# A graph and expert kernel: the gate moves into the second graph layer, and lots are gathered from lists instead of scattered to a buffer

## The reference

```python
x = x + _L0_gnn_ref(_layernorm(x), edge_index, edge_type_8, ...)   # two rgcn layers, relu between
x = x + _L0_ffn_ref(_layernorm(x)[None], Wg, bg, W1, b1, W2, b2)[0]

gate_logits = xf @ Wg + bg
top_w, top_i = jax.lax.top_k(gate_logits, 2)
top_w = jax.nn.softmax(top_w, axis=-1)
for e in range(E):                       # E = 8, H = 1024
    h = jax.nn.gelu(xf @ W1[e] + b1[e], approximate=False)
    out = out + w_dense[:, e:e + 1] * (h @ W2[e] + b2[e])
```

## Time and profile before

| what | us |
|---|---|
| median of 3 runs | 2932.98 (2931.1 to 2933.84) |
| span of the profiled execution | 3487.9 |
| setup and layer 1, until its last tile is out | 1383 |
| layer 2, until its last tile is out | 2665 |
| first matmul of the first lot | 2861 |
| end of the expert stage | 3488 |

### The profile page before, as it was taken

One profiled execution on the slowest core, in us unless ns is written; L12 is line 12 of the kernel. 1 busy time (PEld: TensorE's weight loads), 2 busy tenths in 40 slices (PEclk: granted clock), 3 DMA queues, 4 the chain that ended last, 5 costly groups with the idle time before them and its releaser, 6 DMA issues.

```text
span 3487.9 us, 82172 instructions
## 1 busy us (share of the span) xinstructions
PE 2472.0 (71%) x19212; PEld 1832.7 (53%) x19213; DVE 1780.8 (51%) x4984; ACT 1225.2 (35%) x2344; POOL 1862.5 (53%) x1980
## 2 busy tenths in 40 slices
PE   1346787678687786346776587687877428999999
PEld 0113565356365564114564365465656327888887
DVE  7324455345355454124454354354545338787777
ACT  5202343134243342012343143152432126555554
POOL 1666566655655554666556656655563543333333
PEclk9557999589799898557998798798997559999999
DMA  6223323233332232223333333333335234322222
GB/s 216 80 83 112 88 87 91 85 87 89 87 88 87 86 89 64 86 84 97 98 104 97 94 100 99 94 105 95 101 100 163 102 115 132 96 73 71 71 70 59
DMA packets 165489, 333.24 MB, mean 96 GB/s; under 512 B 36078, under 2 KB 102346, under 8 KB 165288
## 3 DMA queue, kind: packets, MB, share of 16 engines
q0 software_dynamic: 91632, 247.48, 24.1%
q1 hardware_dynamic: 39912, 41.03, 4.0%
q10 hardware_dynamic: 33872, 43.92, 3.9%
HBM read 285.39 MB, written 49.07 MB: 96 GB/s over the span
## 4 chain that ended last, share of the span: by engine, by line
PE 44%; issue 22%; DVE 10%; another core or an unknown queue 9%; DVEq 7%; SPq 2%; ACT 2%; DMA 1%; ACTq 0%; POOLq 0%; POOL 0%
PE more_banks L1408 13%; PE sum_banks L1384 9%; PE sum_banks L1385 7%; PE more_banks L1535 4%; PE sum_banks L1535 3%; PE more_banks L1400 3%; PE sum_banks L1545 3%; DVEq L1044 3%; DVEq L1041 2%; DVE sels L1044 2%; DVEq L1027 1%; DVE stage L1079 1%; DVE sels L1036 1%; PE sum_banks L1426 1%
## 5 line engine op out<-in xcount | busy, mean ns | idle before, releaser
L509 POOL DMA_INDIRECT ring<-table,tabs x1584 | 1526.9, 964 | 1046.4 <-SPq L399 670.0
L1384 PE MATMUL sum_banks<-ring,sels 128*128 x2348 | 726.6, 311 | 630.1 <-issue 420.1
L1408 PE MATMUL more_banks<-weights,stage 128*128 128x256 f16 x5292 | 919.1, 290 | 22.0 <-issue 21.4
L1385 PE MATMUL sum_banks<-ring,sels 128*128 x2348 | 732.2, 313 | 41.5 <-issue 38.7
L1384 PEld LDWEIGHTS sum_banks<-ring,sels 128*128 128x128 f16 (+1 forms) x2348 | 242.4, 103 | 928.2 <-issue 896.9
L683 ACT ACTIVATE stage<-sum_banks,inv 128x256 f16<-128x256 f32 x784 | 328.1, 473 | 789.5 <-issue 384.9
L1408 PEld LDWEIGHTS more_banks<-weights,stage 128*128 128x128 f16 x5292 | 531.1, 104 | 135.3 <-issue 37.1
L1036 DVE SCALAR_TENSOR_TENSOR sels<-lane,win_off,tabs 128x256 f16<-128x256 f16 x792 | 349.4, 482 | 422.1 <-remote 181.9
L654 ACT ACTIVATE stage<-more_banks 128x1024 f16<-128x1024 f16 x392 | 402.0, 1026 | 419.1 <-remote 405.6
L1044 DVE TENSOR_SCALAR sels<-lane,win_off,tabs 128x128 f16 x780 | 260.6, 334 | 495.8 <-issue 339.6
L1079 DVE SCALAR_TENSOR_TENSOR stage<-sum_banks,inv,stage 128x256 f16<-128x256 f32 x784 | 347.0, 479 | 57.2 <-issue 40.2
(11 more groups left out here) (319 smaller groups left out, 2407.5 us busy)
## 6 DMA issues: line engine op xcount, KB each, us to landing
ring<-table,tabs POOLq DMA_INDIRECT x1584
weights<-L_ffn_W ACTq DMA_DIRECT2D x96, 178.5 KB
stage<-L_ffn_W ACTq DMA_DIRECT2D x16, 1024.0 KB, 5.0
edge_work<-lot_in SPq DMA_DIRECT2D x54, 260.0 KB
table<-edge_work ACTq DMA_DIRECT2D x49, 128.0 KB
lot_in<-sels SPq DMA_DIRECT2D x8, 260.0 KB
weights<-L_gnn_W SPq DMA_DIRECT2D x2, 1024.0 KB, 8.3
weights<-L_gnn_W ACTq DMA_DIRECT2D x2, 1024.0 KB
```

The costliest lines, as they stand in the source:

```text
L509: pool.indirect_dma_start(ring_rows[:, b % RING, 0:2 * D], None, tables[layer], bass.IndirectOffsetOnAxis(row_tab[:, b:b + 1], 0)).then_in ...
L1384: pe.matmul(to[:, 0:D + 1], hot, ring_row[:, ds(at + D, D + 1)], start=first, stop=last, skip_group_check=True)
L1385: return pe.matmul(to[:, 0:D], hot, ring_row[:, ds(at, D)], start=False, stop=last, skip_group_check=True)
L1408: return [pe.matmul(ps_out[par], rows[:, xp * KD + k, :], w16[:, wp, k, r * D:(r + 1) * D], start=part == PART_ORDER[0] and n == 0, stop=p ...
```

## The change

The scatter and its buffer go. The normed rows are written once, in node order, to `z_dram` by plain transfers, and POOL gathers each lot with two indirect transfers from lists of node numbers. The lists are made on the chip: a place within an expert is split into a low part (0 to 127) and a column; for each of 49 x 2 tile and choice pairs DVE marks both as one-hot matrices, ACT scales one copy by the row in the tile and POOL another by the tile, and PE multiplies them into PSUM (`ps_nth`, `ps_tile`), where the list of node numbers stands.

The rows z, their transposes, the gate product and the logits are made tile by tile inside the loop of layer 2, three to four tiles behind (`gate_tiles` in the place of `graph_tiles`, with four tiles ahead of the loop). Choice and places are done for 45 tiles at once and then for the last 4.

```diff
+        def gate_tiles(eng, body):
+            for t in range(4):
+                body(t, t % 2, t)
+            with eng.Fori(2, PAIRS) as i:
+                body(i * 2, 0, 4)
+                body(i * 2 + 1, 1, 4)
+            body(TILES - 1, 0, 4)
@@ PE, in a couple of layer 2
+                    if layer == 1 and k == 0 and age >= 4:
+                        z_transposes(t - 4, par, 1 - par, t - 2)
                     regs, at, need, end = load_couple(c)
+                    if layer == 1 and k == 2 and age >= 4:
+                        gate(t - 4, par, ps_sum[slot][1][:, GATE_AT:GATE_AT + X])
@@ ACT, in a tile of layer 2
+                            if k == 0 and age >= 3:
+                                deviation(t - 3)
+                            if k == 0 and age >= 4:
+                                z_columns(t - 4, par, 1 - par)
+                            if k == 3 and age >= 3:
+                                act.load([tile_reg], tile_at[0:1, ds(t - 3, 1)])
+                                z_store(t - 3, 1 - par, act.snap(tile_reg, min_val=0, max_val=NP - P), age >= 4)
@@ DVE, in a tile of layer 2
+                            if layer == 1 and k == 2 and h == 1 and age >= 4:
+                                logit_row(t - 4, ps_sum[slot][1][:, GATE_AT:GATE_AT + X])
-                            if k == 3 and age == 2:
-                                v.wait_ge(layer_done, t - 1)
-                                v.bn_stats(flat(bn[:, ds(t - 2, 1), :]), flat(acc[:, ds(t - 2, 1), :])).then_inc(bn_done, 1)
+                            if k == 1 and age >= 3:
+                                z_row(t - 3, 1 - par, age >= 4)
+                            if k == 3 and age >= 2:
+                                row_stats(t - 2)
@@ DVE, after the layer: the marks of a chunk of 7 tiles (14 pairs), WIDE[c] = 56 * (c + 1)
+            def pick_places(c):
+                if c >= 2:
+                    v.wait_ge(listed, c - 1)
...
+                v.scalar_tensor_tensor(low_hot[c % 2], lane16[:].unsqueeze(1).to_broadcast([P, PAIRED, P]), 0.0, low, ALU.add, ALU.is_equal).then_inc(places_marked, 1)
...
+                v.scalar_tensor_tensor(high_hot(c), col_no[:, 0:WIDE[c]].unsqueeze(1).to_broadcast([P, PAIRED, WIDE[c]]), 0.0, high, ALU.add, ALU.is_equal).then_inc(places_marked, 1)
@@ PE, after the layer
+            def list_rows(c):
...
+                for i in range(PAIRED):
+                    at_high = high_hot(c)[:, i, 0:WIDE[c]]
+                    pe.matmul(ps_nth[:, 0:WIDE[c]], low_part[c % 2][:, i, :], at_high, start=False, stop=False, skip_group_check=True)
+                    ins = pe.matmul(ps_tile[:, 0:WIDE[c]], low_tile[c % 2][:, i, :], at_high, start=False, stop=False, skip_group_check=True)
+                ins.then_inc(listed, 1)
@@ POOL
-                    for k in range(2):
-                        pool.indirect_dma_start(lot_in, bass.IndirectOffsetOnAxis(pos[0:rows, k, t:t + 1], 0),
-                                                z_group[c % GROUPS][0:rows, i, :], None).then_inc(scattered[c % GROUPS], 16)
+                pool.tensor_tensor(low_tile[c % 2].rearrange("p (t k) n -> p t (k n)", t=CHUNK), low_hot[c % 2].rearrange("p (t k) n -> p t (k n)", t=CHUNK),
+                                   node_tile[:, c * CHUNK:(c + 1) * CHUNK].unsqueeze(2).to_broadcast([P, CHUNK, 2 * P]), ALU.mult).then_inc(tile_scaled, 1)
...
+            def take_ids(ids, listed_ids, n, copies):
...
+                pool.tensor_copy(ids[:], listed_ids[:, ds(col, HALVES)]).then_inc(packed, 1)
+                pool.wait_ge(packed, copies + (2 * X + 1))
+            def gather_lot(n, copies):
+                take_ids(next_ids, lot_rows_of, n, copies)
...
+            def next_lot(n, copies):
+                pool.wait_ge(tags_taken, n)
+                gather_lot(n, copies)
...
                     with pool.Fori(0, rest) as j:
-                        store_new(start + j)
+                        next_lot(start + j + 2, (start + j) * 3 + 4)
+                        store_new(start + j, (start + j) * 3 + 5)
                         fetch_old(start + j + 1)
                         landed(start + j)
```

More of the change, by code:

```diff
@@ L741, in _, with soft @@
[L741 to L748 removed]
+            def soft(n, first, last):
+                act.wait_ge(gap_ready, n + 1)
+                act.activation(gap[:, first:last], gap[:, first:last], ACT.Exp).then_inc(exp_ready, 1)
@@ new lines, in _, with choose @@
+            link(v.memset(most[:, 3:4], 0.0))
+            def choose(n, first, last):
+                rows, count = slice(first, last), last - first
+                expert = experts.to_broadcast([P, count, X])
+                here = logits[:, rows, :]
+                for k in range(2):
+                    hot, pick, least = choice[:, k, rows, :], picks[:, k, rows, :], chosen[:, rows, k]
+                    link(v.tensor_reduce(top[:, k, rows], here, AX.X, ALU.max))
+                    link(v.tensor_tensor(pick, here, top[:, k, rows].unsqueeze(2).to_broadcast([P, count, X]), ALU.is_equal))
+                    link(v.scalar_tensor_tensor(pick, expert, float(-X), pick, ALU.add, ALU.mult))
+                    link(v.tensor_reduce(least, pick, AX.X, ALU.min))
```

640 lines of the change are left out of this document (383 added, 257 removed).

## The result

The changed kernel takes 3133.39 us (median of 4 runs, 3132.95 to 3134.26) against 2933.41 us before: a ratio of 1.0681, 95% interval 1.0666 to 1.0696. It is 200 us slower. The forecast was 2899 us.

What follows compares the result with a forecast made beforehand. It took layers 1 and 2 as bound by no engine alone, the gate stage by POOL's scatter chain, the lots by PE. Gate stage -82, layer 2 +28 and lots +20 gave -34 from 2932.98: 2899 us, range 2838 to 2972.

Steps and rivals of the forecast that it cites:

- layer 2, moved work: Layer 2: added transposes, gate products and small DVE operations cost +28 us, between 0 and 140.
- rival 2: Layer 2: DVE's loop of 331 instructions no longer stays resident and is fetched each round; +40, 2940 us, chance 0.10.
- gate stage: Between layer 2 and the first lot: new chain replaces the scatters, -97 us profiled, -82 us unprofiled.
- lots: Expert stage: POOL's round of 11.2 us just equals PE's pace; +20 us, between 0 and 85, 106 at profiled rates.
- rival 1: Expert stage: POOL becomes the bound at its profiled rate; lots +106 us, kernel 2985 us, chance 0.20.
- But profiled rates can't all hold in the unprofiled run: POOL's transfers, expert stage: the unprofiled run is 555 us shorter, so the transfer pitch must be below 1.24 us.
- the sum of 965 us of other stretches: Whole kernel: time with no layer gather running, 84, 31, 27, 196 and 627 us, used to bound the gather pitch.
- the pitch of 1.08: POOL's transfers, unprofiled: 1.08 us taken instead of 1.28, making POOL's round in the lots 11.2 us.
- the 13.3 us of the round by profiled rates: Expert stage: POOL's round with six transfers and three copies takes 13.3 us, more than the 11.3 us of a lot.
- The rule that stood beside it: DVE's layer-2 loop: engines hold two blocks of 256 instructions; old loop lies in two, new one in three.
- The sum of 100 us: Gate stage: the new chain of choice, places, marks, lists and first gathers takes 100 us, against 196.5 before.
- DVE's marks hide POOL's product: Gate stage: POOL's product for a chunk, 2.9 to 5.7 us, lies under DVE's 3.3 to 8.6 us of marks.

Runs made afterwards that it cites:

- the disturbed execution: First profile of the unchanged kernel before: 3487.9 us, against a median of 2933 us without the profiler.
- the undisturbed profile: Second profile of the unchanged kernel before: 2933.16 us, span 2931.1 us.
- the copies with 60 memsets: Changed kernel with 60 memsets on DVE ahead of layer 2, plus two copies of 256 numbers on DVE per layer-2 tile: 3138.86 us.
- the plain loop with 100: Changed kernel with 100 one-number memsets on DVE ahead of layer 2, its loop otherwise as in the change: 3128.41 us.

## Why the prediction was wrong, point by point

It forecast 2899 us (2838 to 2972) and faster with 0.72. Its terms beside what was measured:

| term | forecast | measured | how |
|---|---|---|---|
| layer 2, moved work | +28 | +29 | 855.6 - 826.5, loop resident |
| layer 2, instruction fetches | none (rival 2: +40, chance 0.10) | +103 | 958.4 - 855.6 |
| gate stage | -82 | -35 | 130.9 - 165.7 |
| lots | +20 (rival 1: +106, chance 0.20) | +102 | 714.7 - 613.1 |

The miss of 234 us is thus 103 of fetches that the sum put at nothing, 82 of the lots and 47 of the gate stage, and 2 of the rest.

- **The lots.** The step that failed is "But profiled rates can't all hold in the unprofiled run". They do: the gather and its gap are 0.946 and 0.30 us in an execution of 2931.1 us. I had set the sum of 965 us of other stretches, taken from the disturbed execution, against the median of undisturbed ones; in the undisturbed profile they are 84 + 23 + 16 + 160 + 613 = 896 us, and the waits of 670 us that I thought had to shrink with the pitch shrank by themselves to 87. The bound was also too tight by its own rows: I had put a gap of 0.30 us behind each of the 1584 gathers, and in the view of the earlier trace rows the line of these gaps is `issue: 326.2, 1005`. With the 1526.9 us that the gathers are busy that makes 1853 us, not 1980, and 1853 + 965 = 2818 leaves 115 us for waits at the full rates. So the pitch of 1.08 was wrong, the 13.3 us of the round by profiled rates were near the 12.87 measured, and rival 1's 106 us near the 102. The lot it is compared with is 10.93 us, not 11.3. That removing the drain gives 85 of them back shows that POOL's round, not the landing of the rows, set the pace.
- **The fetches.** The sum had nothing for them. Rival 2 named the mechanism and the place, but not the price: it took 50 to 100 us on DVE, half of it hidden. DVE's idle time for issue ahead of its marks grew by 62 us, in that range, but none of it was hidden: its waits for PE grew by 33 us beside it, with PE's granted clock at 0.91 against 0.96, and the layer grew by 103. The rule that stood beside it, blocks of 256 of which two are held (the Trainium skill, Runtime: NRT & Kernel Launch, Instruction fetch mechanics), foretold that the new loop would be fetched and the old one not. Its blocks are not borne out: the packets are 8 KB, and loops within two such blocks (the copies with 60 memsets, and the plain loop with 100) were fetched in every round. The measurement decides: three packets of 128 and one ahead fit all positions. That a packet of 8 KB is 128 instructions is an estimate from the page's 256 in 16 KiB; three and one ahead are then its 512. What the page says of sequential fetching ahead and of a taken branch out of what is held agrees with the packets that come again in every round.
- **Layer 2's work.** The size was right, the reason not, so that the size is luck. I had given 23 us to PE's transposes and gate product; the transposes made twice cost nothing, the gate product was not tried. 9 us are the place of DVE's statistics, ahead of the register load, and 20 stay open.
- **The gate stage.** Both ends were off. The sum of 100 us counts from the end of PE's last product of layer 2. From there the stage before takes 159.9 us (2158.1 to 2318.0) and not the 177 that I had left of 196.5. After, the chain takes 125.0 (2291.4 to 2416.4), 25 more than summed. The step that failed is that DVE's marks hide POOL's product: it costs 21 of them. Its bound of 2.9 to 5.7 us came from a cast with one input and nothing beside it, and its best row (3.2) agrees; that the same size can take 14.0 us next to DVE I had not looked for. The 16 copies of the lists took 8.5 us (2398.5 to 2407.0) against 6.5. The mark of 1792 numbers (2.0 us against 2.2) and the eight of `prepare` (5.4 against 6) were as predicted.
- **The range** was built on independent rivals. Two of them came true at once, which with 0.2 x 0.1 I had not put in at all; even so, both at their own prices, -82 + 28 + 106 + 40, give 3025 us, still 108 short. (The upper end of the forecast's own range, 2933 - 82 + 45 + 45, is 2941 and not 2935, which changes nothing here.)

## What to carry to other kernels

A profiled execution that is 19% longer than the median is not slower in everything by 19%: look at which rows are longer (here waits, while POOL's transfers and their gaps were the same) before scaling any price, and take a second profile. When transfers are added to an engine's round, sum the round with every gap, copy and drain at the rates of the rows and set it against the period; here a round 2 us over the period became 100 us, and one drain was most of the difference. Where a change lengthens a loop with many instructions, its length and place in the engine's stream are part of the change, and the count of instruction packets in that stretch tells at once whether it stays resident. Work moved to an idle engine is free only if the two engines don't hold each other up: compare the rows of one size beside each other.

## What the runs showed of the hardware

- DVE's loop over two tiles is fetched again in each round, or not at all, by its place: 115 or 116 instruction packets of 8 KB in layer 2 against 10 or 11, and 950 to 962 us against 854 to 859 (846 and 848 with the statistics moved). Twenty one-number memsets ahead of it were worth 98 us (one execution).
- Behind the pause of 1427 to 1430 us, in which PE did nothing, its granted clock was 0.67 and 0.76 for two stretches of 3 us, then 1.00 again; over layer 2 it was 0.91 with these pauses and 0.96 without.
- An indirect transfer on POOL costs 0.85 to 1.0 us of idle time behind a copy that it waits for, against 0.30 us behind another transfer.
- The drain at the end of POOL's round delayed the next copy to 2.5 us behind the last transfer, against 0.4 us without it.
- POOL's product of 1792 numbers took 3.2 us alone and 3.8 to 14.0 beside DVE's marks, and ended 3.03 to 3.04 us behind the last of them. Operations of DVE on 4 to 45 numbers took 2.58 to 3.14 us beside the product, and 0.17 to 0.18 when it was on ACT.
